# Weight quotients computed on GpSimd in float32 in a cross-attention and MX feed-forward kernel, with a new VectorE order and later weight loads from GpSimd's queue

## What is computed

```python
def _L0_xattn_ref(teacher_logits, teacher_features, Wq, bq, Wk, bk):
    query = jnp.einsum('bnc,dc->bnd', teacher_features, Wq) + bq
    key = jnp.einsum('bnc,dc->bnd', teacher_features, Wk) + bk
    energy = jnp.einsum('bnd,bmd->bnm', query, key)
    attention = jax.nn.softmax(energy, axis=-1)
    return jnp.einsum('bln,bmn->blm', teacher_logits, attention)

def mx_quant(x):                      # blocks of 32 along the last axis
    xb = x.reshape(s[:-1] + (s[-1] // BLOCK, BLOCK))
    amax = jnp.max(jnp.abs(xb), axis=-1, keepdims=True)
    shared_exp = jnp.floor(jnp.log2(jnp.where(amax > 0, amax, 1.0)))
    scale = jnp.exp2(shared_exp - (BITS - 2))
    q = jnp.clip(jnp.round(xb / scale), -2.0 ** (BITS - 1), 2.0 ** (BITS - 1) - 1) * scale
...
x = bf16_round(inputs); residual = x
h = mx_layernorm(x, ln_w, ln_b)
h = mx_linear(h, W1, b1)              # quantises h and W1 [2048, 512]
h = mx_gelu(h)
h = mx_linear(h, W2, b2)              # quantises h and W2 [512, 2048]
...
x = x + _L0_xattn_ref(_layernorm(x, axis=-1), ctx_1024, ...)
x = x + _L0_ffn_ref(_layernorm(x, axis=-1), ...)
```

## Time and profile before

| | us |
|---|---|
| median of 3 runs | 290.87 (290.16 to 291.86) |
| the profiled execution | 291.86 |
| its span | 290.0 |
| busy in it: DVE, PE, ACT, POOL | 252.4, 228.2, 168.8, 81.2 |

### The profile page before, as it was taken

The page is one execution under the profiler, slowest core; times in us unless marked ns, Lnnn a source line. Parts: engine busy times, 40 slices in busy tenths (PEclk is TensorE's granted clock), DMA queues, the critical chain, the costliest instruction groups (busy, mean ns, idle before and its releaser), DMA issues.

```text
span 290.0 us, 3187 instructions
## 1 busy us (share of the span) xinstructions
PE 228.2 (79%) x907; PEld 95.2 (33%) x916; DVE 252.4 (87%) x369; ACT 168.8 (58%) x287; POOL 81.2 (28%) x104
## 2 busy tenths in 40 slices
PE   1386739985998259633699789899999989999882
PEld 0232223432343024211244333344444434444330
DVE  2349999999898899999979999699999999999950
ACT  1218416546895456945986699856655656655300
POOL 1092020022004500043150130841323333444453
PEclk9999798998699959875999999999999999999999
DMA  6996993989778941949652044565453376744851
GB/s 172 379 385 226 222 261 63 239 234 197 137 208 210 205 95 36 214 84 175 110 65 46 0 90 93 100 154 126 88 123 84 86 162 135 155 110 95 162 123 72
DMA packets 103077, 42.92 MB, mean 148 GB/s; under 512 B 93844, under 2 KB 96152, under 8 KB 102552
## 3 DMA queue, kind: packets, MB, share of 16 engines
q1 hardware_dynamic: 99024, 32.78, 54.7%
q10 hardware_dynamic: 3560, 9.97, 10.3%
q0 software_dynamic: 480, 0.02, 0.1%
HBM read 15.48 MB, written 4.19 MB: 68 GB/s over the span
## 4 chain that ended last, share of the span: by engine, by line
DVE 39%; PE 26%; ACT 12%; issue 7%; DMA 7%; POOL 4%; SPq 3%; POOLq 0%; DVEq 0%; ACTq 0%
DVE amax L746 10%; PE ps L649 8%; PE ps L694 6%; PE ps L706 4%; DVE vw L932 3%; DVE w_int L789 3%; DMA cx<-in_ctx 3%; DVE hq L937 3%; DVE pf L853 3%; ACT phl L560 3%; DVE wquant L843 2%; SPq L239 2%; PE ps L652 2%; ACT wst L556 2%; PE ps L629 2%
## 5 line engine op out<-in xcount | busy, mean ns | idle before, releaser
L649 PE MATMUL ps<-pT,xT 128*128 128x512 f16 x192 | 50.4, 419 | 13.7 <-DMA pT<-phl 11.3
L694 PE MATMUL ps<-w1T,cxT 128*128 128x512 bf16 x256 | 58.0, 380 | 0.0
L706 PE MATMUL ps<-w2T,xhl 128*128 128x512 bf16 x247 | 56.7, 380 | 1.6 <-issue 1.0
L556 ACT ACTIVATE wst<-ps 128x1024 bf16<-128x1024 f32 x32 | 32.3, 1019 | 26.1 <-PE ps L694 26.1
L746 DVE TENSOR_REDUCE amax<-phl 128x64 f32<-128x2048 bf16 x16 | 36.5, 2281 | 4.3 <-ACT phl L560 4.3
L649 PEld LDWEIGHTS ps<-pT,xT 128*128 128x128 f16 x192 | 20.3, 107 | 48.1 <-issue 32.4
L416 POOL TENSOR_TENSOR wst<-wst,vs 128x512 bf16<-128x512 bf16 x16 | 18.5, 1158 | 60.4 <-DVE wquant L848 30.8
L637 PE MATMUL ps<-qkT 128*128 128x512 f32 x32 | 18.8, 694 | 20.1 <-ACT pf L457 16.0
L706 PEld LDWEIGHTS ps<-w2T,xhl 128*128 128x128 bf16 x256 | 23.7, 98 | 30.8 <-issue 3.6
L694 PEld LDWEIGHTS ps<-w1T,cxT 128*128 128x128 bf16 x256 | 23.7, 98 | 30.1 <-issue 3.6
L560 ACT ACTIVATE phl<-wst 128x2048 bf16<-128x2048 bf16 x16 | 30.6, 1911 | 1.3
(11 more groups left out here) (75 smaller groups left out, 345.8 us busy)
## 6 DMA issues: line engine op xcount, KB each, us to landing
wst<-in_L_ffn_W ACTq DMA_DIRECT2D x8, 1024.0 KB, 7.3
out_x<-wst SPq DMA_DIRECT2D x16, 256.0 KB, 2.9
xs<-in_x SPq DMA_DIRECT2D x3, 1024.0 KB, 13.9
cx<-in_ctx SPq DMA_DIRECT2D x4, 512.0 KB, 6.8
xs<-in_x ACTq DMA_DIRECT2D x1, 1024.0 KB, 9.0
xhl<-pf SPq DMA_TRANSPOSE x17, 4.3
lnw<-in_L_ffn_ln_w ACTq DMA_DIRECT2D x1, 256.0 KB, 16.0
lnb<-in_L_ffn_ln_b ACTq DMA_DIRECT2D x1, 256.0 KB, 15.8
```

Of the source, the lines that this page charges most:

```text
L556: act.activation(ys[:, k, 1024 * g:1024 * g + 1024], ps_y[:, 2 * g:2 * g + 2, :], ACT.Copy)\
L649: pe.matmul(ps_pv[:, t % 2, :], xT[:, t, NT * a + n, :], pT[:, :, NT * c + n, :], start=(s == 0), stop=False)
L694: last = pe.matmul(ps_y[:, c, :], h1T[:, k, t, :], w1T[:, 4 * c:4 * c + 4, t, :], start=False, stop=(t == KT - 1))
L706: last = pe.matmul(ps_z[:, k, :], h2T[:, k, t, :], w2T[:, t, :], start=False, stop=(t == FT - 1))
```

## The change

The weights' quotient leaves DVE. Pool computes it in place in `wst`, in float32, as `over_scale`; DVE's clip then reads float32 from `wst` and writes int16. So `wst` is free for the next unit only after the clip, and the weight chain has six steps on DVE's semaphore instead of seven. `w_inverse`, which releases Pool's quotient, is moved: W2's of unit b - 1 to the very start of `front(b)`, ahead of `w_amax(W1, b)` and two `negmax`; W1's to the middle, ahead of `negmax(b, 2)`, `w_amax(W2, b)` and two of the moments, which are taken apart into pairs. All weight loads but the first two go from ACT's queue to Pool's. `back` keeps only `times_w` and `plus_b`, and runs only after fronts 2 and 3.

```diff
-W_STEPS = 7
+W_STEPS = 6
...
+            def over_scale(a, u):
+                pool.wait_ge(w_step[a], W_STEPS * u + 4)
+                w = blocks(wst[:, a, :])
+                inverse = mxi[:, a, :, 0:1].broadcast_to([P, NB, BLOCK])
+                pool.tensor_tensor(w, w, inverse, ALU.mult).then_inc(w_u[a], 1)
+            def load_w1(u):
+                pool.wait_ge(w_step[W1], W_STEPS * (u - 1) + 5)
+                pool.dma_start(wst[:, W1, :].rearrange("p (r k) -> p r k", r=4), w1_t[u]).then_inc(ld_next[W1], 16)
+            def load_w2(u):
+                pool.wait_ge(w_step[W2], W_STEPS * (u - 1) + 5)
+                pool.dma_start(wst[:, W2, :], w2_t[u]).then_inc(ld_next[W2], 16)
...
+            over_scale(W1, 0)
             factors_x(1)
+            load_w1(1)
             def batch(b, x, v):
+                over_scale(W2, b)
+                load_w2(b + 1)
+                over_scale(W1, b + 1)
                 if x is not None:
                     factors_x(x)
+                if b + 2 < B:
+                    load_w1(b + 2)
                 if v is not None:
                     factors_v(v)
...
+            over_scale(W2, B - 1)
             factors_v(B - 2)
...
-                    if t == 2 and b is not None:
-                        load_w2(front)
...
-                if not isinstance(front, int) or front + 1 < B:
-                    load_w1(front + 1)
...
             def w_amax(a, u):
-                dve.wait_ge((ld_w1, ld_w2)[a], 16 * (u + 1))
+                if u == 0:
+                    dve.wait_ge((ld_w1, ld_w2)[a], 16)
+                else:
+                    dve.wait_ge(ld_next[a], 16 * u)
...
-            def w_over(a, u):
-                dve.wait_ge(w_step[a], W_STEPS * u + 4)
-                inverse = mxi[:, a, :, 0:1].broadcast_to([P, NB, BLOCK])
-                dve.tensor_tensor(blocks(w_int[:, :]), blocks(wst[:, a, :]), inverse, ALU.mult)\
-                   .then_inc(w_step[a], 1)
             def w_clip(a, u):
-                dve.wait_ge(w_step[a], W_STEPS * u + 5)
-                dve.tensor_scalar(w_int[:, :], w_int[:, :], QMAX, None, ALU.min).then_inc(w_step[a], 1)
+                dve.wait_ge(w_u[a], u + 1)
+                dve.tensor_scalar(w_int[:, :], wst[:, a, :], QMAX, None, ALU.min).then_inc(w_step[a], 1)
             def w_mult(a, u):
                 wait(dve, (w1T_rdy, w2T_rdy)[a], 16 * u)
-                dve.wait_ge(w_step[a], W_STEPS * u + 6)
+                dve.wait_ge(w_step[a], W_STEPS * u + 5)
...
+            def x_moments(b, t):
+                dve.wait_ge(ld_x[b], 16)
+                dve.bn_stats(stats[:, t, :], xs[:, LT * b + t, :]).then_inc(st, 1)
             def x_stats(b):
-                if isinstance(b, int):
-                    dve.wait_ge(ld_x[b], 16)
-                for t in range(LT):
-                    dve.bn_stats(stats[:, t, :], xs[:, LT * b + t, :]).then_inc(st, 1)
-                if isinstance(b, int) and b > 0:
+                if b > 0:
                     dve.wait_ge(rx_rdy, b)
+                    dve.wait_ge(xn_rdy, LT * b)
                 for t in range(LT):
                     wait_alone(dve, st, LT * b + (t + 1), dve_gate)
...
-            def front(b, w1, w2, stats_next, h1):
+            def front(b, stats_next, h1):
+                if b > 0:
+                    w_inverse(W2, b - 1)
+                    w_amax(W1, b)
                 negmax(b, 0)
+                negmax(b, 1)
+                if b > 0:
+                    w_power(W1, b)
+                    w_clip(W2, b - 1)
                 normalise(b, 0)
-                if w1 is not None:
-                    w_amax(W1, w1)
-                negmax(b, 1)
+                if b > 0:
+                    w_scale(W1, b)
                 normalise(b, 1)
                 recip(b, 0)
-                if w1 is not None:
-                    w_power(W1, w1)
+                if b > 0:
+                    w_mult(W2, b - 1)
                 recip_scaled(b, 0)
-                if w1 is not None:
-                    w_scale(W1, w1)
                 x_low(b, 0)
-                if w1 is not None:
-                    w_inverse(W1, w1)
+                recip(b, 1)
+                p_low(b, 0)
+                recip_scaled(b, 1)
+                x_low(b, 1)
+                w_inverse(W1, b)
+                negmax(b, 2)
+                w_amax(W2, b)
+                if stats_next is not None:
+                    x_moments(stats_next, 0)
+                    x_moments(stats_next, 1)
                 if h1 is not None:
                     h1_amax(h1)
-                negmax(b, 2)
+                w_power(W2, b)
                 normalise(b, 2)
-                recip(b, 1)
+                recip(b, 2)
+                if stats_next is not None:
+                    x_moments(stats_next, 2)
+                    x_moments(stats_next, 3)
+                recip_scaled(b, 2)
+                w_scale(W2, b)
+                p_low(b, 1)
+                negmax(b, 3)
+                normalise(b, 3)
+                x_low(b, 2)
+                if stats_next is not None:
+                    x_stats(stats_next)
+                w_clip(W1, b)
                 if h1 is not None:
                     h1_power(h1)
-                recip_scaled(b, 1)
-                p_low(b, 0)
+                recip(b, 3)
+                p_low(b, 2)
                 if h1 is not None:
                     h1_scale(h1)
-                x_low(b, 1)
+                recip_scaled(b, 3)
+                x_low(b, 3)
+                w_mult(W1, b)
                 if h1 is not None:
                     h1_inverse(h1)
-                if w2 is not None:
-                    w_over(W2, w2)
-                negmax(b, 3)
-                normalise(b, 3)
-                recip(b, 2)
+                p_low(b, 3)
                 if h1 is not None:
                     h1_over(h1)
-                recip_scaled(b, 2)
-                p_low(b, 1)
-                x_low(b, 2)
-                if h1 is not None:
                     h1_clip(h1)
-                if w2 is not None:
-                    w_clip(W2, w2)
-                    w_mult(W2, w2)
-                recip(b, 3)
-                p_low(b, 2)
-                recip_scaled(b, 3)
-                x_low(b, 3)
-                w_over(W1, b)
-                if stats_next is not None:
-                    x_stats(stats_next)
-                if h1 is not None:
                     h1_mult(h1)
-            def back(b, w1, w2, tail):
-                w_amax(W2, w2)
-                p_low(b, NT - 1)
-                w_power(W2, w2)
-                if tail is not None:
-                    times_w(tail, 0)
-                w_scale(W2, w2)
-                if tail is not None:
-                    plus_b(tail, 0)
-                w_inverse(W2, w2)
-                if tail is not None:
-                    for t in range(1, LT):
-                        times_w(tail, t)
-                        plus_b(tail, t)
-                w_clip(W1, w1)
-                w_mult(W1, w1)
+            def back(tail):
+                for t in range(LT):
+                    times_w(tail, t)
+                    plus_b(tail, t)
...
             split3(b2_step, b2f, b2p)
+            for t in range(LT):
+                x_moments(0, t)
             x_stats(0)
             w_amax(W1, 0)
             w_power(W1, 0)
             w_scale(W1, 0)
-            w_inverse(W1, 0)
-            front(0, None, None, 1, None)
-            back(0, 0, 0, None)
-            for b in range(2, B):
-                dve.wait_ge(ld_x[b], 16)
+            front(0, 1, None)
+            front(1, 2, None)
             dve.wait_ge(ld_ln, 32)
-            front(1, 1, 0, 2, None)
-            back(1, 1, 1, None)
-            front(2, 2, 1, 3, None)
-            back(2, 2, 2, 0)
-            for b in range(3, B):
-                front(b, b, b - 1, None, b - 3)
-                back(b, b, b, b - 2)
+            front(2, 3, None)
+            back(0)
+            front(3, None, 0)
+            back(1)
+            w_inverse(W2, B - 1)
```

8 lines of the change are left out of this document (1 added, 7 removed).

## The result

| | before | changed |
|---|---|---|
| time, median | 290.93 us (290.16 to 291.86, 4 runs) | 308.36 us (306.88 to 309.31, 4 runs) |
| ratio | | 1.060, 95% interval 1.057 to 1.064 |
| span of the profiled execution | 290.0 us | 306.7 us |
| first h2 maximum on DVE | 155.18 us | 170.18 us |
| second first-layer product on PE | 150.53 us | 166.24 us |

The kernel is slower, as forecast: 308.4 us against a predicted 304.0, within the range of 291 to 314. Some executions of one kernel run over 1.5% longer than its fastest; the ratios in this document leave these out and the medians do not, which shows above all in e12_cliplate (304.1 and 304.3 us of its four runs) and e3_actloads (306.9 of its five).

What follows compares the result with a forecast made beforehand. DVE was taken to pace the attention half, up to the first h2 maximum. Terms summed to +15.8 us there, less 2.8 absorbed later; the ACT chain gave +13.1: 290.9 + 13.1 = 304.0 us, range 291 to 314.

Steps and rivals of the forecast that it cites:

- quotients leave DVE: Eight float32 weight quotients move off DVE, the clip costing 0.5 us more each: -13.6 us of DVE work.
- W1 loads: DVE stands 5.3 us before the W1 maxima of units 1 and 2, loads being released late: +10.6 us.
- W2 loads: DVE waits 2.0 us for W2's load in each of units 1, 2 and 3: +6.0 us.
- Pool against DVE: Pool's quotients and DVE's two-input instructions take turns, so DVE waits behind the maxima: +3.5 us.
- order, ACT late: normalise(b, 2) moves behind W2's maximum and load wait; ACT's queue runs late and DVE waits at p_low: +5.0 us.
- Pool's small results: DVE waits longer for Pool's factors at back(0), back(1) and batch 2's tail: 7.7 less today's 3.4, +4.3 us.
- Clip and Pool's instruction: Prices assumed: DVE's float32 clip 1.2 us, Pool's float32 quotient of 2048 elements 4.0 us.
- slow clip: Rival: the float32 clip runs at 1.04 ns an element, 8.5 us more, 312 us; chance 0.05.
- slow queue: Rival: 1 MB loads from Pool's queue take 10 us to land, 15 us more, 319 us; chance 0.08.
- The load wait covers that here: W2's unit 1 quotient queues on Pool behind factors_x1(0), waiting for ACT's squares; DVE's load wait was to hide this.
- The second half: After 155 us PE and DVE share the bound; 2.8 of DVE's 15.8 us vanish in a gap, leaving +13.0.
- the other chain: Over ACT to PE's second product: v_sums 17.0 us late, less 3.9 us of slack, +13.1 us.

Runs made afterwards that it cites:

- e12_cliplate: e1_spare with normalise(b, 2) ahead of W2's maximum, and W2's clip and multiply moved down behind x_low(b, 1); median 302.7 us.
- e3_actloads: The changed kernel with its six later weight loads issued from ACT's queue, right after the clips, instead of Pool's; median 303.2 us, ratio to before 1.035.
- e1_spare: The changed kernel with W1's load ahead of factors_x and Pool's quotient written to its own tile, so loads need not wait for the clip; 299.3 us.
- e8_offload: The kernel before, its order and ACT-queue loads kept, with only the eight quotients moved to Pool, into one spare tile; 304.5 us, ratio 1.042.

## Why the prediction was right, point by point

The direction, the main cause and the first h2 maximum were right: +15.8 us forecast there, +15.0 measured. The time rose by 17.4 us where 13.1 was forecast. The terms, as the prediction put them:

| term | forecast | measured |
|---|---|---|
| quotients leave DVE | -13.6 | -13.4 (17.6 gone, 8 x 0.52 for the clip) |
| W1 loads | +10.6 | +14.2 (8.7 and 5.4) |
| W2 loads | +6.0 | +1.1 |
| Pool against DVE | +3.5 | +1.9, and +3.7 at the clip that I had counted as covered |
| order, ACT late | +5.0 | +6.5 |
| Pool's small results | +4.3 | +3.8 |
| PE's energies | not in the sum | -2.8 (2.0 against 4.8) |
| first h2 maximum | +15.8 | +15.0 |

That the sum came so close is in part luck: the W1 loads, the clip's wait and ACT were 8.8 us worse than forecast, and the W2 loads, Pool's turns, its small results and PE's energies 9.8 us better.

- **Clip and Pool's instruction.** 1.21 us against my 1.2; 3.63 against my 4.0. The neighbouring rows were good guides, and the rivals of a slow clip and a slow queue fall.
- **W1 loads, mis-sized.** I took `factors_x` at the 1.7 us of the earlier trace rows, behind the clip. With DVE's clip, p_low, x_low and multiply beside it, it took 3.6 in the fronts that mattered (34.78 to 38.41), so that the load was issued 2.7 us behind the clip, and the first load landed in 9.6 us instead of 7.0. Of the 3.4 us by which the first wait exceeded my 5.3, about 1.0 is Pool's and 2.6 the landing; the second wait, 5.4, was as forecast. The mechanism, late release behind the clip and `factors_x`, is shown by e1_spare.
- **W2 loads, mis-sized the other way.** 7.0 us to landing was a middle of two medians; these took 5.1 to 5.9, and the cover, which I had counted as 5.1 us, was 5.3, 5.8 and 5.8. A term of the form landing minus cover with both near 5 to 7 us has an error as large as itself.
- **A step that failed.** "The load wait covers that here", of W2's quotient behind `factors_x1(0)`. The load wait ended at 76.37; ACT's squares, late as well, released the factors only at 78.37, and the quotient started at 79.97, behind the maximum and the two `negmax` that it should have run under. The clip's wait for it cost 3.7 us, and 5.3 in the runs where the load wait was cut: two waits that overlapped, of which the second shows when the first is taken away.
- **The second half failed as a term.** I let 2.8 us vanish in a gap of DVE, and gave the other chain 3.9 us of slack by comparing `v_sums` with PE's second product. That product starts straight behind PE's own work, whose first part is released by the transposes of the last p_low ([9.36 <-DMA pT<-phl]). In all fourteen traces the span is the second product plus 139.2 to 143.2 us: 139.2 to 140.8 in the six where the fourth product took 3.63 us, 140.4 to 143.2 in the eight where it was slow, five of them with the late slow product besides. So nothing was absorbed: +15.7 there, and 1.0 more with the fourth product at the lower clock, 16.7 in the span.
- **What I missed altogether** is why the order was changed at all. In e8_offload, without it, 20.9 us go to held instructions; I had priced the ports for the new places only.
